# Message order by halves of the probabilities, new engine orders, and the second half's diagonal matrices on GpSimd, in an attention-like step before a dequantized feed-forward block

## What is computed

```python
def _layernorm(x, axis=-1, eps=1e-05): ...
def _L0_attn_ref(x):                      # per position l: 4x4 scores over n
    q = jnp.transpose(x, (2, 0, 1))
    scores = jnp.einsum('lnc,lmc->lnm', q, q) / jnp.asarray(c, x.dtype) ** 0.5
    prob = jax.nn.softmax(scores, axis=-1)
    msg = jnp.einsum('lnm,lmc->lnc', prob, q)
    return x + jnp.transpose(msg, (1, 2, 0))
def _L0_ffn_ref(x, ...):                  # NF4 weights, HD = 1024, M = 3584
    g = jnp.einsum('bsh,mh->bsm', x, Wg)
    u = jnp.einsum('bsh,mh->bsm', x, Wu)
    return jnp.einsum('bsm,hm->bsh', jax.nn.silu(g) * u, Wd)
x = x + _L0_attn_ref(_layernorm(x, axis=-1))
x = x + _L0_ffn_ref(_layernorm(x, axis=-1), ...)
```

## Time and profile before

| | us |
|---|---|
| median of 3 runs (1658.64 to 1658.76) | 1658.72 |
| the profiled execution's own time | 1659.08 |
| its span | 1657.3 |
| PE busy | 1628.3 (98%) |
| DVE busy | 1204.0 (73%) |
| ACT busy | 1032.5 (62%) |
| POOL busy | 61.5 (4%) |

### The profile page before, as it was taken

How to read it: one execution, slowest core, us unless ns; L and a number is a source line. 1 busy time by engine, 2 the same in 40 slices (tenths; PEclk the granted TensorE clock), 3 DMA queues, 4 the chain that set the end, 5 groups by cost and what they waited for, 6 DMA issues and landing times.

```text
span 1657.3 us, 20221 instructions
## 1 busy us (share of the span) xinstructions
PE 1628.3 (98%) x7906; PEld 788.1 (48%) x7906; DVE 1204.0 (73%) x1542; ACT 1032.5 (62%) x1122; POOL 61.5 (4%) x98
## 2 busy tenths in 40 slices
PE   6899999999999999999999999999999999999999
PEld 6864444444444444444444444444444444444444
DVE  7988967685766768576676857677977667577566
ACT  5679676776777677677767767788986526352000
POOL 4252000000000000000000000000000000000000
PEclk9999999999999999999999999999999999999999
DMA  6330232332423233142323324234764444343773
GB/s 271 128 153 14 96 121 96 114 130 68 143 84 130 96 112 132 68 143 83 131 96 112 132 69 143 83 134 156 258 251 177 151 151 176 126 176 126 254 254 131
DMA packets 77183, 226.39 MB, mean 137 GB/s; under 512 B 5280, under 2 KB 20256, under 8 KB 76576
## 3 DMA queue, kind: packets, MB, share of 16 engines
q1 hardware_dynamic: 77088, 225.10, 37.9%
HBM read 156.93 MB, written 68.16 MB: 136 GB/s over the span
## 4 chain that ended last, share of the span: by engine, by line
PE 93%; DVE 3%; ACT 2%; POOL 1%; issue 1%; DMA 0%; POOLq 0%; SPq 0%; DVEq 0%; ACTq 0%
PE ps L1659 20%; PE ps L1661 20%; PE ps L1660 20%; PE ps L1796 10%; PE ps L1797 10%; PE ps L1798 10%; PE ps L1600 2%; PE ps L1629 1%; POOL xb L643 1%; DVE stats L1005 1%; ACT codes L678 1%; PE ps L1613 0%; PE ps L1638 0%; DMA xa<-x_dram 0%; DVE xb L1173 0%
## 5 line engine op out<-in xcount | busy, mean ns | idle before, releaser
L678 ACT ACTIVATE codes<-codes 128x1024 f32<-128x1024 f32 (+1 forms) x672 | 708.9, 1056 | 148.0 <-DMA codes<-q_dram 134.0
L1466 DVE SCALAR_TENSOR_TENSOR xb<-ps,y_back,xb 128x512 f32<-128x512 f32 x139 | 103.1, 749 | 71.8 <-PE ps L1798 67.7
L1659 PE MATMUL ps<-xb,rw 128*128 128x512 f16 x388 | 147.1, 379 | 0.7 <-ACT gs L766 0.7
L1659 PE MATMUL ps<-xa,wg 128*128 128x512 f16 x388 | 147.1, 379 | 0.3 <-DVE xa L1185 0.3
L1660 PE MATMUL ps<-xa,wg 128*128 128x512 f16 x388 | 147.1, 379 | 0.0
L1661 PE MATMUL ps<-xa,wg 128*128 128x512 f16 x388 | 147.1, 379 | 0.0
L1659 PE MATMUL ps<-xa,rw 128*128 128x512 f16 x388 | 147.1, 379 | 0.0
L1660 PE MATMUL ps<-xa,rw 128*128 128x512 f16 x388 | 147.1, 379 | 0.0
L1661 PE MATMUL ps<-xa,rw 128*128 128x512 f16 x388 | 147.1, 379 | 0.0
L1659 PE MATMUL ps<-xb,wg 128*128 128x512 f16 x388 | 147.1, 379 | 0.0
L1660 PE MATMUL ps<-xb,wg 128*128 128x512 f16 x388 | 147.1, 379 | 0.0
(11 more groups left out here) (293 smaller groups left out, 2922.2 us busy)
## 6 DMA issues: line engine op xcount, KB each, us to landing
codes<-q_dram SPq DMA_DIRECT2D x84, 512.0 KB, 4.7
absm<-a_dram SPq DMA_DIRECT2D x69, 512.0 KB, 3.8
h_dram<-rw SPq DMA_DIRECT2D x28, 1024.0 KB, 4.2
gs<-h_dram SPq DMA_DIRECT2D x21, 1344.0 KB, 5.9
h_dram<-rw SPq DMA_DIRECT2D x28, 768.0 KB, 4.7
rw<-h_dram SPq DMA_DIRECT2D x11, 896.0 KB, 5.3
rw<-x_dram SPq DMA_DIRECT2D x16, 512.0 KB, 11.1
xa<-a_dram SPq DMA_DIRECT2D x13, 512.0 KB, 5.4
```

The costliest lines, as they stand in the source:

```text
L678: fn(real, real if step else whole, ACT.Prelu, bias=at0, scale=slope, alpha=left).then_inc(bends_done, 1)
L1466: return v.scalar_tensor_tensor(out=dst, in0=ps[:, bank, :], scalar=y_back[:, 0:1], in1=dst, op0=ALU.mult, op1=ALU.add)
L1659: mm(dst, w_hi, x_hi, start=(start and kt == 0), stop=False, skip_group_check=True)
```

## The change

It does the following.

- `message_order` sets which (c, g) is step k: first groups 0 to 3 of row tiles 0 and 1 (k = 0 to 7), then groups 4 to 7 of both (k = 8 to 15), then row tiles 2 and 3 in full. `tile_messages` is the number of additions after which a row tile is whole: 12, 16, 24, 32.
- Quarter 2 of the diagonal matrices goes from DVE to POOL, with a semaphore `d_third` of its own, ahead of quarter 3.
- DVE's list: the additions of steps 4 to 7 stand ahead of `scale_codes(0)`; steps 8 to 15 alternate with the statistics of row tile 0; `weight_low(0)` and `scale_codes(1)` stand after step 10, `weight_low(1)` after step 17; the statistics of row tile 2 and 3, `x_low`, `scale_codes(2)`, `scale_codes(3)`, `norm_scales` and `weight_low` take new places; in the last eight steps the addition stands ahead of `x_low`.
- PE: `transpose_xn` of tiles 0 to 7 stands after `messages` of the same step, not before it.
- ACT: `load_silu`, one activation of one element for each partition after step 11, and new places for `bends`, `w_high` and `silu_of_half(0)`.
- POOL: `normalized` of tiles 24 to 27 no longer waits for `x1_out[2]`, for all messages and for `scaled` 4; tiles 28 to 31 still wait for the last two.

```diff
+        message_order = ([(c, g) for f in range(2) for c in range(2) for g in range(LG // 2 * f, LG // 2 * f + LG // 2)]
+                         + [(c, g) for c in range(2, CT) for g in range(LG)])
+        tile_messages = [1 + max(k for k in range(CT * LG) if message_order[k][0] == c) for c in range(CT)]
...
-                sp.wait_ge(x1_ready, LG * (c + 1))
+                sp.wait_ge(x1_ready, tile_messages[c])
...
-            spread_prob(1)
-            spread_prob(3)
+            spread_prob(1, d_pool)
+            spread_prob(2, d_third)
+            spread_prob(3, d_pool)
...
-            pool.wait_ge(x1_out[2], 16)
+            for k in range(24, 28):
+                pool.wait_ge(t2_done, 21 + (k - 24))
+                normalized(k)
             pool.wait_ge(m_done, CT * LG)
             pool.wait_ge(scaled, 4)
-            for k in range(24, 32):
-                if k < 28:
-                    pool.wait_ge(t2_done, 21 + (k - 24))
+            for k in range(28, 32):
                 normalized(k)
...
+            def load_silu():
+                fn(first_silu[:, :], plus_half[:, 0:1], ACT.Silu, bias=0.0, scale=1.0)
...
-            for g in range(LG):
-                copy_yt(0, g)
-            copy_yt(1, 0)
-            copy_yt(1, 1)
+            for k in range(10):
+                copy_yt(k)
             exp_half(1)
-            copy_yt(1, 2)
+            copy_yt(10)
+            copy_yt(11)
+            load_silu()
+            copy_yt(12)
             bend(1, 4)
-            copy_yt(1, 3)
-            bends(1, range(5, NB))
-            copy_yt(1, 4)
+            copy_yt(13)
+            copy_yt(14)
+            bend(1, 5)
+            copy_yt(15)
+            bend(1, 6)
+            copy_yt(16)
             w_high(0)
...
+            copy_yt(17)
+            bend(1, 7)
+            for k in range(18, 23):
+                copy_yt(k)
+            w_high(1)
+            for k in range(23, 31):
+                copy_yt(k)
+                bend(2, k - 23)
+            copy_yt(31)
             for k in range(8):
                 x_blocks(k)
             bends(3, range(0, 2))
...
-            w_high(2)
+            bends(3, range(4, 6))
             x_blocks(14)
             x_blocks(15)
-            bend(3, 4)
+            bend(3, 6)
             x_blocks(16)
             x_blocks(17)
-            silu_of_half(0)
+            w_high(2)
+            bend(3, 7)
             x_blocks(18)
             x_blocks(19)
-            bends(3, range(5, NB))
-            x_blocks(20)
-            x_blocks(21)
+            silu_of_half(0)
             w_high(3)
-            x_blocks(22)
-            x_blocks(23)
+            for k in range(20, 24):
+                x_blocks(k)
...
             turn_prob(1)
-            spread_prob(1)
+            for k in range(4, 8):
+                add_message(k)
             scale_codes(0)
-            for g in range(4, LG):
-                add_message(0, g)
-            weight_low(0)
-            scale_codes(1)
...
+            for k in range(8, 16):
+                add_message(k)
+                dve.wait_ge(x1_ready, 4 if k < 12 else 12)
+                row_stats(CT, 2 * (k % 4) + (k - 8) // 4)
+                if k == 10:
+                    weight_low(0)
+                    scale_codes(1)
+            row_sums(CT)
+            dve.wait_ge(x1_ready, tile_messages[1])
+            for k in range(16, 24):
+                add_message(k)
+                row_stats(CT + 1, k - 16)
+                if k == 17:
                     weight_low(1)
-                    norm_scales()
-            for g in range(LG):
-                x_low(g)
-                add_message(3, g)
-            dve.wait_ge(x1_ready, LG * 3)
-            for half in range(2 * B):
+            row_sums(CT + 1)
+            for k in range(24, 32):
+                add_message(k)
+                x_low(k - 24)
+            dve.wait_ge(x1_ready, tile_messages[2])
+            for half in range(B):
+                row_stats(CT + 2, half)
+            x_low(8)
+            x_low(9)
+            for half in range(B, 2 * B):
                 row_stats(CT + 2, half)
             row_sums(CT + 2)
-            x_low(8)
-            x_low(9)
-            scale_codes(2)
             x_low(10)
             x_low(11)
-            dve.wait_ge(x1_ready, LG * 4)
+            scale_codes(2)
+            norm_scales()
+            x_low(12)
+            x_low(13)
+            dve.wait_ge(x1_ready, tile_messages[3])
             for half in range(B):
                 row_stats(CT + 3, half)
-            x_low(12)
-            x_low(13)
-            row_stats(CT + 3, B)
-            row_stats(CT + 3, B + 1)
             x_low(14)
             x_low(15)
-            row_stats(CT + 3, B + 2)
-            row_stats(CT + 3, B + 3)
+            for half in range(B, 2 * B):
+                row_stats(CT + 3, half)
             row_sums(CT + 3)
+            x_low(16)
+            x_low(17)
             weight_low(2)
-            for k in range(16, 20):
+            scale_codes(3)
+            x_low(18)
+            x_low(19)
+            weight_low(3)
+            for k in range(20, 24):
                 x_low(k)
...
-                    pe.wait_ge(d_pool if g // 2 % 2 else d_dve, 1 + g // 4)
+                    pe.wait_ge((d_dve, d_pool, d_third, d_pool)[g // 2], 1 + g // 6)
...
+            for k in range(CT * LG):
+                if k == 4:
+                    repeat_prob(1)
+                messages(k)
+                if k + LG < CT * LG:
+                    transpose_y(k + LG)
+                else:
+                    transpose_xn(k + LG - CT * LG)
```

More of the change, by code:

```diff
@@ L626, in _, with spread_prob @@
             g.tensor_tensor(norm2[:, :], norm2[:, :], plus_half[:, :], ALU.pow).then_inc(norm_root, 1)
-            def spread_prob(quarter):
+            def spread_prob(quarter, done):
                 pool.wait_ge(prob_m_ready, B * (quarter // 2 + 1))
@@ L635, in spread_prob @@
                                 mask32[:, None, :].broadcast_to([P, LB // 4 * B, 32]),
-                                ALU.mult).then_inc(d_pool, 1)
-            spread_prob(1)
-            spread_prob(3)
+                                ALU.mult).then_inc(done, 1)
+            spread_prob(1, d_pool)
+            spread_prob(2, d_third)
+            spread_prob(3, d_pool)
             def normalized(k):
@@ L720, in x_blocks @@
                     act.wait_ge(x1_out[0], 16)
-                    act.wait_ge(d_dve, 2)
+                    act.wait_ge(d_dve, 1)
+                    act.wait_ge(d_third, 1)
                     act.wait_ge(d_pool, 2)
@@ L1326, in _ @@
             scale_codes(0)
-            for g in range(4, LG):
-                add_message(0, g)
-            weight_low(0)
-            scale_codes(1)
-            for c in (1, 2):
-                dve.wait_ge(x1_ready, LG * c)
-                for g in range(LG):
-                    add_message(c, g)
-                    row_stats(CT + c - 1, g)
-                row_sums(CT + c - 1)
-                if c == 1:
-                    weight_low(1)
-                    norm_scales()
-            for g in range(LG):
-                x_low(g)
-                add_message(3, g)
@@ L1363, in _ @@
             row_sums(CT + 3)
+            x_low(16)
+            x_low(17)
             weight_low(2)
-            for k in range(16, 20):
-                x_low(k)
-            scale_codes(3)
-            x_low(20)
-            x_low(21)
-            weight_low(3)
-            x_low(22)
-            x_low(23)
+            scale_codes(3)
[3 more added lines that the diff above has]
+            for k in range(20, 24):
+                x_low(k)
             t_sums(0, 0)
@@ L1603, in _, with transpose_y @@
                         last.then_inc(gram_done, 1)
[L1605 to L1606 removed]
+            def transpose_y(k):
+                c, g = message_order[k]
                 if k == 0:
@@ L1615, in transpose_y, with messages @@
                 last.then_inc(t_done, 1)
-            def messages(c, g):
-                k = LG * c + g
+            def messages(k):
+                c, g = message_order[k]
                 pe.wait_ge(t_read, k + 1)
                 if c == 0:
-                    pe.wait_ge(d_pool if g // 2 % 2 else d_dve, 1 + g // 4)
+                    pe.wait_ge((d_dve, d_pool, d_third, d_pool)[g // 2], 1 + g // 6)
                 if k >= LG + 2:
@@ L1628, in messages @@
                     lb = 4 * g + b
-                    last = mm(bank[:, :, b, :], y_t[:, lb, :], d_mat[lb // 16][:, lb % 16, :, :], start=True, stop=True)
+                    last = mm(bank[:, :, b, :], y_t[:, 4 * (k % LG) + b, :], d_mat[lb // 16][:, lb % 16, :, :], start=True, stop=True)
                 last.then_inc(m_done, 1)
@@ L1732, in p7 @@
                 product(s, S3, XT3, s % 2, False).then_inc(p7_done, 1)
-            for g in range(2):
-                transpose_y(0, g)
+            for k in range(2):
```

(16 more changed lines are left out.)

38 lines of the change are left out of this document (13 added, 25 removed).

## The result

The changed kernel takes 1648.07 us (median of six, 1647.51 to 1648.23) against 1658.29 us of the kernel before beside it; the ratio is 0.9937, 95% interval [0.9927, 0.9948], so 10.2 us less. A second set of runs gave 1648.30 against 1658.82 us, 0.9937 [0.9924, 0.9949]. The forecast was 1647.8.

What follows compares the result with a forecast made beforehand. PE bounds the kernel, busy 1628.3 of 1657.3 us. Gains of 5.7 (messages), 5.0 (parts 0 and 1) and 0.2 (parts 2 and 3) sum to 10.9 us, giving 1647.8 us, range 1644.3 to 1653.0.

Steps and rivals of the forecast that it cites:

- The pool of lost time: From `repeat_prob(1)` to product part 4: 104.2 us hold 89.2 of PE work, so at most 15.0 us to gain.
- Step 4 and the clock: Messages: step 4 starts at 57.1 without its 2.4 us wait, and the full clock saves 1.7 us more.
- GpSimd's two quarters: POOL's spreading of quarters 2 and 3: 1.8 us each taken, up to 2.95; ready at 60.1 and 61.9.
- Additions beside GpSimd: DVE's additions 4 to 7 beside POOL's spreading: taken as not held, 0.69 us each; upper bound 3.3 us of delay.
- The waits that stay: PE's remaining waits: steps 14 and 21, first normalized tile, tiles 15, 17, 19, 21 and 29; 0.1 to 1.2 us each.
- the walk: Stepping through the new engine lists with handoffs from rows: part 0 at 95.9, part 2 at 125.0, part 4 at 150.4 us.
- GpSimd's sharing in parts 2 and 3: POOL's tiles 28 to 31 take 3.0 us plus 1.4 for sharing with DVE; `t_sums(0,1)` then starts at 131.1.
- its slack relative to PE unchanged: Behind part 4: later work keeps its slack, since DVE's `t_low(0,3)` comes 11.0 us earlier too; no loss charged.
- Held additions: Rival: additions beside POOL's spreading are held, or sharing costs more; gain 7 us, 1651.7 us; chance 0.15.
- the first stall alone: Rival: only step 4's stall goes, 2.4 + 1.7 = 4.1 us, giving 1654.6 us; chance 0.07.
- all waits gone: Rival: every PE wait between `repeat_prob(1)` and part 4 goes, 15.0 us, giving 1643.7 us; chance 0.05.
- a falling clock at short waits: Rival: each of nine short PE waits left brings a clock fall, 15.4 us in all, giving 1663 us; chance 0.06.

Runs made afterwards that it cites:

- x1: Changed kernel with the message steps again row tile by row tile, the third quarter staying on GpSimd; 1653.65 us, ratio 0.9970 to the kernel before.
- x2: Changed kernel with `scale_codes(0)` again ahead of additions 4 to 7; median 1651.55 us, ratio 0.9950 to the kernel before.
- x7: Changed kernel with six PSUM banks for messages of steps 8 to 19, and `x_low(16)`, `x_low(26)`, `x_low(28)`, `x_blocks(26)` moved; 1647.34 us, ratio 0.9933.
- x10: Changed kernel with `transpose_xn` again ahead of `messages` in the last eight steps; 1649.29 us, ratio 0.9942 to the kernel before.
- x6: Changed kernel up to part 0 of the products, then ACT, DVE and GpSimd lists as before, except `norm_scales` behind `scale_codes(2)`; 1652.42 us, ratio 0.9960.
- x5: Changed kernel with quarter 2 of the diagonal matrices made by DVE again, behind `turn_prob(1)`; 1648.83 us, ratio 0.9939 to the kernel before.

## Why the prediction was right, point by point

- *The pool of lost time.* PE's pure work was counted as 89.2 us; what the changed kernel needs above it and `repeat_prob(1)` (0.84) is 4.7 us. The view of waits has 2.8 of it; counted by starts, the eight places below lose 4.3, and 0.4 has no place. (The 24.9 us for 28 message groups go by 0.89 us a group; the 0.90 that is stated would give 25.2.)
- *Step 4 and the clock.* As predicted, no wait and a full clock. x1 and x2 show both halves: the wait and the fall of the clock come back with either edit, in x2 in the execution that has a profile.
- *GpSimd's two quarters* take 3.79 us together, 1.9 each, near the 1.8 taken and far from the 2.95 of the earlier trace rows; the reading of that row, that 1.1 us of it were DVE's own spreading, is what x2 shows at work.
- *Additions beside GpSimd* last 0.69 us, the lower bound; the first `scale_codes` 1.28.

Timelines of POOL and of DVE in the changed kernel:

```profile
57.14 3.79 POOL L641 TENSOR_TENSOR xb<-gs,mask 128x1024 f32<-128x1024 f32 x2 [6.12 <-DVE gs L1073]
```

```profile
57.09 0.69 DVE L1187 TENSOR_TENSOR xb<-ps,xb 128x512 f32<-128x512 f32 x1
58.36 0.69 DVE L1187 TENSOR_TENSOR xb<-ps,xb 128x512 f32<-128x512 f32 x1 [0.58 <-PE ps L1647]
...
61.63 1.28 DVE L1094 SCALAR_TENSOR_TENSOR tmp<-codes,w_scale,absm 128x1024 f32<-128x1024 f32 x1
```

- *The waits that stay* were named with their size, and all are there. Counted alike, by how much later PE starts than its pace allows: step 14 0.54 us (0.6 predicted), step 21 0.68 (0.8), first tile 0.27 (0.3), tile 15 0.40 (0.2), tile 17 0.07 (0.1), tile 19 0.61 (0.5), tile 21 0.29 (0.3), tile 29 1.43 (1.2). The idle times in the rows are smaller, since the row ahead lasts longer than its step to the next start.

```profile
69.78 1.13 PE L1647 MATMUL ps<-xb,gs 128*128 128x128 f32 x8 [0.38 <-DVE xa L1187]
...
79.84 1.13 PE L1647 MATMUL ps<-xb,gs 128*128 128x128 f32 x8 [0.52 <-DVE rw L1187]
...
108.69 0.63 PE L1656 MATMUL ps<-ident,xb 128*128 128x128 f32 x4 [0.24 <-POOL xb L653]
...
116.42 0.63 PE L1656 MATMUL ps<-ident,xb 128*128 128x128 f32 x4 [0.45 <-DVE xb L1199]
...
145.87 0.63 PE L1656 MATMUL ps<-ident,xb 128*128 128x128 f32 x4 [1.26 <-DVE gs L1199]
```

The wait at 108.69 is put down to POOL, but it fits `x_low(12)`, which starts at 107.86 and frees PE 0.83 us later.

- *The half microsecond too much.* Counted from `repeat_prob(1)`, part 0 is 0.2 us, part 2 0.3 and part 4 0.6 us later than in the walk. The mis-sized term with a row is GpSimd's sharing in parts 2 and 3: the prediction put 1.4 us on it, and its last six tiles take 6.41 us where six undisturbed ones take 4.55, so 1.9. `t_sums(0,1)` follows 0.5 us later than predicted, DVE is full from there to `x_low(26)`, which ends the wait of tile 29, and so part 4 is 0.6 late. The 0.3 us ahead of part 2 have no single term: tiles 15 and 19 wait 0.3 longer than predicted, and steps 14 and 21 0.2 less. (By the walk's own part 4 the gain is 161.38 - 150.4 = 11.0; the sum by stages has 10.9.)

```profile
123.96 6.41 POOL L653 TENSOR_SCALAR xb<-rw,ln_scale,ln_bias 128x512 f32<-128x512 f32 x6 [1.22 <-PE ps L1656]
```

- *The step that was wrong though it cost nothing*: "its slack relative to PE unchanged", argued from the 1.62 us that DVE waited for PE. That is DVE's slack. ACT's first copy behind it had 0.2 us: x7 brings PE 2.4 us earlier to part 4 but the copy only 1.1, and PE waits 1.08 there. The forecast stood because that copy came as much earlier as PE, 10.4 us against the kernel before (140.70 and 151.10 us after `repeat_prob(1)`). The argument did not look at it, so this was luck; of 1.3 us more on PE alone, 1.1 would have been lost.
- *What the gain is made of*, from the sums of x1 to x10: the order of steps 4.7 us, the additions ahead of the codes 4.0 (2.9 by the medians), `w_high(2)`'s place 6.9, the transposes behind the messages 0.9, four statistics first 0.9, the third quarter 0.7, the table load 0. They add up to far more than 10.4: the first two bring back the same kind of stall, and the third brings one of 5.79 us that the kernel before never had. So these are the prices of taking an edit back in the changed kernel, not shares of the gain; no run adds one edit to the kernel before. The prediction gave the gain by stage, which x6 shows to add up within 0.8 us; by part it gave no shares.
- *The rivals.* Held additions, the first stall alone, all waits gone, and a falling clock at short waits all fell. (The last counts nine waits, the walk names eight. The 3.3 us for a rule without the distinction of inputs belong to the first rival, not the second.) As to the clock: behind the scores, waits of up to 1.58 us were followed by full speed in all of these kernels, those of 2.24, 2.37, 3.10 and 5.79 us by the lower level, for 3 to 4 us of PE's work each.

## What to carry to other kernels

Where each engine runs a fixed list, read the gain of a reordering by walking the lists with start-to-start times and handoffs taken from rows, and count the pure work of the bounding engine first: it gives the most that any order can bring. Ask of every instruction that is moved whether its input is there when the engine comes to it: one `w_high` issued 6 us too early cost two thirds of the whole gain. Slack has to be read for each engine that hands to the bounding one, not only for the busiest of them.

## What the runs showed of the hardware

- A DVE instruction that reads two SBUF tensors and a GpSimd instruction of the same kind took turns, whole instructions at a time. Which goes first can't be read from the starts in the profile: DVE's row began 0.05 us before GpSimd's in x2 and was served second (3.04 us instead of 1.28), it began 0.05 us before in x5 and 0.04 in the kernel before and was served first (GpSimd's 2.95 instead of 1.9). In x2 it was `scale_codes`, in the other two `spread_prob`; whether that or a chance of the moment decides is open. DVE's additions from PSUM beside the same GpSimd instruction kept their 0.69 us.
- Moving an activation table load by 62 us changed nothing that the span shows, in a kernel where ACT is busy for nine tenths of the time around it. In another order of ACT's list (x6) the rows put 0.8 us down to it: what it costs is a matter of the cover behind it.
